# h turned by a transposing DMA in place of TensorE, six slots for the split halves, and a scalar operand for the bound on y

## What is computed

```python
h = jnp.maximum(_layernorm(x, axis=-1), 0.0)          # x: (6144, 128)
anchor_adj = jnp.einsum('md,de,ne->mn', h, weight, input)
scores = jnp.where(adj > 0, anchor_adj, NEG_PAD)      # adj: (6144, 6144) int32
atten = jax.nn.softmax(scores / TEMPERATURE, axis=1)
return x + atten @ input                              # input: (6144, 128)
```

## Time and profile before

| | us |
|---|---|
| median of three runs | 934.15 |
| the profiled execution | 933.88 |
| its span, first to last instruction | 932.1 |
| PE busy | 914.1 (98%) |
| DVE busy | 820.8 (88%) |
| ACT busy | 747.8 (80%) |
| POOL busy | 660.8 (71%) |

### The profile page before, as it was taken

The page is one execution under the profiler, slowest core; times in us unless marked ns, Lnnn a source line. Parts: engine busy times, 40 slices in busy tenths (PEclk is TensorE's granted clock), DMA queues, the critical chain, the costliest instruction groups (busy, mean ns, idle before and its releaser), DMA issues.

```text
span 932.1 us, 25954 instructions
## 1 busy us (share of the span) xinstructions
PE 914.1 (98%) x7611; PEld 663.4 (71%) x7611; DVE 820.8 (88%) x1670; ACT 747.8 (80%) x1511; POOL 660.8 (71%) x449
## 2 busy tenths in 40 slices
PE   7979999999999999999999999999999999999997
PEld 4457777777777777777777777777777777777776
DVE  7988889888988898888988899889888888888885
ACT  5858878888888888888888888888888888888885
POOL 5998677767776776677677767776777677767712
PEclk9999999999999999999999999999999999999999
DMA  9789999999999999999999999999999999999955
GB/s 348 224 219 247 274 250 282 268 259 276 256 272 264 267 268 267 264 262 267 268 263 269 260 269 270 267 256 269 269 269 250 275 270 267 254 267 270 267 99 99
DMA packets 347401, 239.51 MB, mean 257 GB/s; under 512 B 308848, under 2 KB 327408, under 8 KB 328944
## 3 DMA queue, kind: packets, MB, share of 16 engines
q1 hardware_dynamic: 340176, 235.92, 98.0%
q10 hardware_dynamic: 7200, 3.28, 1.3%
HBM read 160.50 MB, written 3.15 MB: 176 GB/s over the span
## 4 chain that ended last, share of the span: by engine, by line
PE 94%; DVE 3%; DMA 2%; issue 1%; ACT 0%; POOLq 0%; POOL 0%; SPq 0%; DVEq 0%; ACTq 0%
PE ps_s L842 39%; PE ps_o L889 26%; PE ps_o L891 13%; PE ps_t L865 13%; DMA pT_dma<-split 1%; DVE probs L643 1%; PE ps_t L908 1%; PE ps_s L918 1%; PE ps_s L835 1%; DVE v L710 1%; DVE pT_lo L666 0%; DMA nodes_raw<-in_L_gnn_input_dram 0%; DVE split L672 0%; PE ps_o L908 0%; ACT yT_hi L544 0%
## 5 line engine op out<-in xcount | busy, mean ns | idle before, releaser
L643 DVE CUSTOM_DVE_ANT_0 probs<-ps_s,absent 128x1024 f32<-128x1024 f32 x288 | 351.5, 1221 | 43.6 <-PE ps_s L842 38.5
L415 POOL TENSOR_SCALAR absent<-present 128x2048 bf16<-128x2048 bf16 x143 | 299.2, 2092 | 66.6 <-DVE chunk_max L643 40.2
L406 POOL TENSOR_SCALAR present<-adj_i 128x2048 bf16<-128x2048 int32 x144 | 272.7, 1894 | 31.1 <-DMA adj_i<-in_adj_dram 25.8
L539 ACT ACTIVATE pT_hi<-ps_t 128x512 f16<-128x512 f32 x281 | 167.7, 597 | 145.7 <-PE ps_t L865 145.5
L889 PE MATMUL ps_o<-v,pT_dma 128*128 128x256 f16 x1152 | 221.0, 273 | 2.0 <-DMA pT_dma<-split 1.9
L507 ACT ACTIVATE ps_t<-probs,neg_max,exp_scale 128x512 f32<-128x512 f32 x285 | 220.4, 773 | 2.5 <-DVE neg_max L653 1.2
L666 DVE TENSOR_TENSOR pT_lo<-ps_t,pT_hi 128x512 f16<-128x512 f32 x284 | 194.5, 685 | 28.7 <-ACT pT_hi L539 28.0
L842 PE MATMUL ps_s<-yT_hi,hT_hi 128*128 128x512 f16 x576 | 218.6, 380 | 1.1 <-DVE chunk_max L643 0.9
L842 PE MATMUL ps_s<-yT_lo,hT_hi 128*128 128x512 f16 x576 | 218.7, 380 | 0.0
L889 PE MATMUL ps_o<-v,pT_hi 128*128 128x256 f16 x1152 | 206.2, 273 | 5.4 <-DVE v L710 4.6
L891 PE MATMUL ps_o<-v,pT_dma 128*128 128x128 f16 x1152 | 205.6, 219 | 0.0
(11 more groups left out here) (81 smaller groups left out, 608.7 us busy)
## 6 DMA issues: line engine op xcount, KB each, us to landing
adj_i<-in_adj_dram SPq DMA_DIRECT2D x144, 1024.0 KB, 5.3
pT_dma<-split SPq DMA_TRANSPOSE x288, 3.4
nodes_raw<-in_L_gnn_input_dram SPq DMA_DIRECT2D x6, 512.0 KB, 6.3
x_res<-in_x_dram SPq DMA_DIRECT2D x48, 64.0 KB, 5.0
out_dram<-fin ACTq DMA_DIRECT2D x48, 64.0 KB, 2.3
x_ln<-in_x_dram SPq DMA_DIRECT2D x46, 64.0 KB, 5.0
x_ln<-in_x_dram ACTq DMA_DIRECT2D x2, 64.0 KB, 3.0
w<-in_L_gnn_weight_dram SPq DMA_DIRECT2D x1, 64.0 KB, 2.1
```

Of the source, the lines that this page charges most:

```text
L406: nc.gpsimd.tensor_scalar(flags(s, c), adj_i[:, c, :], 1.0, 0.0, ALU.min, ALU.max)\
L415: nc.gpsimd.tensor_scalar(by_block(absent[:, c, :]), by_row(flags(s, c)), -ABSENT, ABSENT, ALU.mult, ALU.add).then_inc(absent_done, 1)
L539: nc.scalar.activation(pT_hi[:, p % BANKS, :], turn_area(k, at), ACT.Copy).then_inc(hi_done, 1)
L643: nc.vector.tensor_tensor_reduce(out=probs[:, s, j * SCORE:(j + 1) * SCORE], in0=ps_s[j % 2][:, :], in1=absent[:, c, part * SCORE:(part + ...
```

## The change

h of tiles 0 and 1 is still turned by PE. From tile 2 on POOL makes h with the relu in it (`h_centred`, then `h`), splits it into two fp16 parts (`split_h`, two instructions) and SP turns both parts with one transposing DMA of 256 columns, behind the D halves 2 and 3 of the step, in the queue ahead of the load of adj. PE's scores of tile t+2 wait for that DMA. `turn_h`, `hi_h` and `lo_h` leave the steps. `split` gets six slots, and the waits for a slot change. `y_bound` is made by an operation with a scalar operand.

```diff
+        split = sb("split", [P, D_HALVES, 2, TURN], fp16)
         pT_dma = sb("pT_dma", [P, D_HALVES, 2 * PER_TURN, P], fp16)
-        hT_hi = sb("hT_hi", [P, 2, P], fp16)
-        hT_lo = sb("hT_lo", [P, 2, P], fp16)
+        hT = sb("hT", [P, 2, 2, P], fp16)
+        h_centred = sb("h_centred", [P, 2, D], fp32)
         h = sb("h", [P, 2, D], fp32)
+        h_split = sb("h_split", [P, 2, 2, D], fp16)
         x_ln = sb("x_ln", [P, 2, D], fp32)
         x_res = sb("x_res", [P, 2, D], fp32)
         fin_a = sb("fin_a", [P, 2, D], fp32)
...
             return u * 8 + (16 - 8 * s)
+        def h_turns(u, s):
+
+            return u * 8 - 8 * s
+
         def evac(t, n, at=None):
...
+                sp.dma_start_transpose(pT_dma[:, d, :, :], split[:, d, :, :].rearrange("p s n -> p (s n)"))\
                     .then_inc(turned_in[d], 16)
...
                     turn_d(t, 2, g, late(at, 0, g) if at == LAST else evac(t, g - 2))
+                if has(at, 2):
+
+                    sp.wait_ge(scores_made, t * SCORES + SCORES)
+                    sp.sem_inc(sp_waited, 1)
+                    sp.wait_ge(h_split_done, t + 1)
+                    sp.sem_inc(sp_waited, 1)
+                    sp.dma_start_transpose(hT[:, par, :, :], h_split[:, par, :, :].rearrange("p s n -> p (s n)"))\
+                        .then_inc(hT_in[par], 16)
                 next_adj(0)
...
-            def make_h(u, s, free):
+            def make_h(u, s):
                 pool.wait_ge(aggr_done, u + 1)
                 pool.sem_inc(pool_waited, 1)
                 nc.gpsimd.tensor_scalar(var_eps[:, s, :], mean_var[:, s, 1:2], EPS, H_SCALE ** -2, ALU.add, ALU.mult)\
...
                 nc.gpsimd.tensor_tensor(rstd[:, s, :], var_eps[:, s, :], minus_half[:, :], ALU.pow)\
                     .then_inc(rstd_done, 1)
                 pool.wait_ge(rstd_done, u + 1)
-                if free:
+                pool.sem_inc(pool_waited, 1)
+                nc.gpsimd.tensor_scalar(h_centred[:, s, :], x_ln[:, s, :], mean_var[:, s, 0:1], 0.0,
+                                        ALU.subtract, ALU.max).then_inc(h_centred_done, 1)
+                pool.wait_ge(h_centred_done, u + 1)
+                if isinstance(u, int) and u in (2, 3):
+
                     pool.wait_ge(h_turned, u - 1)
                 pool.sem_inc(pool_waited, 1)
-                nc.gpsimd.tensor_scalar(h[:, s, :], x_ln[:, s, :], mean_var[:, s, 0:1], rstd[:, s, :],
-                                        ALU.subtract, ALU.mult).then_inc(h_done, 1)
+                nc.gpsimd.tensor_scalar(h[:, s, :], h_centred[:, s, :], rstd[:, s, :], 1.0, ALU.mult, ALU.mult)\
+                    .then_inc(h_done, 1)
+
+            def split_h(u, s):
+                pool.wait_ge(h_done, u + 1)
+                if not (isinstance(u, int) and u < 4):
+
+                    pool.wait_ge(hT_in[s], h_turns(u - 2, s))
+                pool.sem_inc(pool_waited, 1)
+                nc.gpsimd.tensor_scalar(h_split[:, s, 0, :], h[:, s, :], 1.0, 1.0, ALU.mult, ALU.mult)\
+                    .then_inc(h_hi_done, 1)
+                pool.wait_ge(h_hi_done, u - 1)
+                nc.gpsimd.tensor_tensor(h_split[:, s, 1, :], h[:, s, :], h_split[:, s, 0, :], ALU.subtract)\
+                    .then_inc(h_split_done, 1)
             def flags(s, c):
...
-                pool.wait_ge(turned_in[(d + BANKS) % D_HALVES], LAST * 16 + (16 if d >= BANKS else 0))
+                pool.wait_ge(turned_in[d], LAST * 16)
                 pool.sem_inc(pool_waited, 1)
-                nc.gpsimd.tensor_scalar(split[:, d % BANKS, 0, :], part, 1.0, 1.0, ALU.mult, ALU.mult)\
+                nc.gpsimd.tensor_scalar(split[:, d, 0, :], part, 1.0, 1.0, ALU.mult, ALU.mult)\
                     .then_inc(split_hi_done, 1)
                 pool.wait_ge(split_hi_done, d // 2 + 1)
-                nc.gpsimd.tensor_tensor(split[:, d % BANKS, 1, :], part, split[:, d % BANKS, 0, :],
+                nc.gpsimd.tensor_tensor(split[:, d, 1, :], part, split[:, d, 0, :],
                                         ALU.subtract).then_inc(split_done, 1)
-            make_h(0, 0, False)
...
-            make_h(2, 0, True)
+            make_h(2, 0)
+            split_h(2, 0)
             v_lo_pool(0)
             pool.wait_ge(absent_done, 4)
...
-                    make_h(t + 3, 1 - par, True)
+                    make_h(t + 3, 1 - par)
+                    split_h(t + 3, 1 - par)
                     convert(t + 3, 1 - par, 0, True)
                 if at == LAST - 1:
...
-                if not (isinstance(u, int) and u < 2):
-                    act.wait_ge(scores_made, u * SCORES - SCORES)
-                nc.scalar.activation(hT_hi[:, s, :], ps_s[s if isinstance(u, int) and u < 2 else 0][:, 0:P],
-                                     ACT.Relu).then_inc(hT_hi_done, 1)
+                nc.scalar.activation(hT[:, s, 0, :], ps_s[s][:, 0:P], ACT.Copy).then_inc(hT_hi_done, 1)
             def exp_p(u, s, c):
                 act.wait_ge(neg_max_done, u + 1)
...
-                if d >= BANKS:
-                    act.wait_ge(turned_in[d - BANKS], u * 16 + 16)
-                elif not (isinstance(u, int) and u == 0):
-                    act.wait_ge(turned_in[d + BANKS], u * 16)
-                nc.scalar.activation(split[:, d % BANKS, 0, :], ps_t[n % BANKS][:, :], ACT.Copy)\
+                if not (isinstance(u, int) and u == 0):
+                    act.wait_ge(turned_in[d], u * 16)
+                nc.scalar.activation(split[:, d, 0, :], ps_t[n % BANKS][:, :], ACT.Copy)\
                     .then_inc(hi_done, 1)
             def v_hi(i):
...
-                            hi_h(t + 2, par)
                         for g in range(1 if at is not None and at + ahead == LAST else 2):
                             hi_d(t + ahead, c, g, CYCLE * z + 2 + g)
-                    elif z == 0 and has(at, 2):
-                        hi_h(t + 2, par)
             steps(act, step)
             act.wait_ge(fin_done, TILES)
...
-                nc.vector.scalar_tensor_tensor(out=hT_lo[:, s, :], in0=area[:, 0:P], scalar=0.0,
-                                               in1=hT_hi[:, s, :], op0=ALU.max, op1=ALU.subtract)\
+                nc.vector.tensor_tensor(hT[:, s, 1, :], area[:, 0:P], hT[:, s, 0, :], ALU.subtract)\
                     .then_inc(hT_lo_done, 1)
...
-                nc.vector.tensor_tensor(split[:, d % BANKS, 1, :], ps_t[n % BANKS][:, :], split[:, d % BANKS, 0, :],
+                nc.vector.tensor_tensor(split[:, d, 1, :], ps_t[n % BANKS][:, :], split[:, d, 0, :],
                                         ALU.subtract).then_inc(turn_freed, 1)
...
-                nc.vector.tensor_tensor(y_bound[:, :], nodes_top[:, :], w_top[:, :], ALU.mult)\
+                nc.vector.tensor_scalar(y_bound[:, :], nodes_top[:, :], w_top[:, :], None, ALU.mult)\
                     .then_inc(y_bound_done, 1)
                 dve.wait_ge(y_bound_done, 1)
...
-                                if has(at, 2):
-                                    lo_h(t + 2, par, ps_s[0])
                                 find_max(t + ahead, (par + ahead) % 2)
                         if q == 0:
                             lo_p(t, CYCLE * z + 1, at)
...
-                part, y, q = ((hT_hi, yT_hi, 0), (hT_hi, yT_lo, 0), (hT_hi, yT_hi, 1), (hT_hi, yT_lo, 1),
-                              (hT_lo, yT_hi, 0), (hT_lo, yT_hi, 1))[i]
+                part, y, q = ((0, yT_hi, 0), (0, yT_lo, 0), (0, yT_hi, 1), (0, yT_lo, 1),
+                              (1, yT_hi, 0), (1, yT_hi, 1))[i]
                 cols = slice(j * SCORE + q * 512, j * SCORE + (q + 1) * 512)
-                made = nc.tensor.matmul(ps_s[j % 2][:, q * 512:(q + 1) * 512], part[:, s, :], y[:, cols],
-                                        start=(part is hT_hi and y is yT_hi), stop=(part is hT_lo))
+                made = nc.tensor.matmul(ps_s[j % 2][:, q * 512:(q + 1) * 512], hT[:, s, part, :], y[:, cols],
+                                        start=(part == 0 and y is yT_hi), stop=(part == 1))
                 if i == 5:
                     made.then_inc(scores_made, 1)
...
-                        pe.wait_ge(hT_lo_done, t + 3)
+                        pe.wait_ge(hT_in[par], h_turns(t + 2, par))
                     for i in range(6):
...
-                    if z == 0 and has(at, 2):
-                        pe.wait_ge(masked, t * SCORES + (SCORES + 5))
-                        turn_h(t + 2, par, ps_s[0])
                     for q in range(2, CYCLE):
                         product(t, par, k + q, at)
```

More of the change, by code:

```diff
@@ L116, in gnn_masked_attention_kernel @@
         pT_lo = sb("pT_lo", [P, BANKS, TURN], fp16)
-        split = sb("split", [P, BANKS, 2, TURN], fp16)
+        split = sb("split", [P, D_HALVES, 2, TURN], fp16)
         pT_dma = sb("pT_dma", [P, D_HALVES, 2 * PER_TURN, P], fp16)
-        hT_hi = sb("hT_hi", [P, 2, P], fp16)
-        hT_lo = sb("hT_lo", [P, 2, P], fp16)
+        hT = sb("hT", [P, 2, 2, P], fp16)
```

(18 more changed lines are left out.)

## The result

The changed kernel takes 972.41 us (median of four runs, 969.99 to 974.99) against 934.0: 1.0403 of before, 95% interval 1.0379 to 1.0427. It is 38 us slower. The forecast was 962, with a range of 943 to 986. The profiled execution took 973.09 us, with a span of 971.3.

What follows compares the result with a forecast made beforehand. PE's own order was taken to bound the kernel. Late landing of h (26.1 us) plus early steps (3) less the bound on y (0.9) gave 28.2 us on 933.88, so 962 us, range 943 to 986.

Steps and rivals of the forecast that it cites:

- What bounds the kernel: Whole kernel: PE is dense in steps of 18.52 us, 0.18 of it for h, and only PE's order sets the steps.
- The new path decides: PE's scores of tile t+2: h lands by DMA 0.58 us late, step 19.10, 26.1 us over 45 steps; own case 0.68.
- The 3 us for early steps: Steps 1 to 6, where the queue is behind and h lands later: 3 us added, out of a possible 8.
- The bounds of the landing: Turning DMA of h, issue to landing: between 1.8 us (order behind the large transpose) and 3.05 us (equal time); 2.15 taken.
- the faster rival: At PE's scores of tile t+2: h lands in time, 9.2 us come off, 925 us; chance 0.09.
- SP's load of adj behind the new DMA: In SP's list: the load of adj is issued at most 0.9 us later, costing nothing while the queue keeps up.
- that rival: The 16 DMA engines become the bound: adj 0.9 us later pushes everything behind it in 46 steps, 41 us, 975; chance 0.12.
- GpSimd: Making and splitting h on GpSimd: 1.1 us more per step, upper end 3.3, hidden by its 2.81 us wait for the mean.
- Slots and bound: Six slots: nothing, as PE does not wait there in dense steps; y_bound with a scalar operand: 0.9 us less.
- The rest of my signs: Expected in the changed profile: PE waits about 0.76 us at first scores, PE's share below 98%, DMA issued 4.8 us after `finish`.

Runs made afterwards that it cites:

- the run with half of adj: The changed kernel with only half of each piece of adj loaded from the fourth tile on, giving the DMA queue slack: 966.3 us, 1.0341 of before.
- the run at 929: The changed kernel with the turning DMA of h issued at the head of SP's step, ahead of the pair for D halves 2 and 3: 929.0 us, 0.9942.
- the run that took 963 us: The changed kernel with h turned by PE as before; the turning DMA stays in its place ahead of adj, into an unread tile: 963.1 us, 1.0318.

## Why the prediction was right, and where it was off

*What bounds the kernel.* Right: PE's order sets the steps, and at 18.35 us a step it does so with h gone from it.

*The new path decides.* Right in mechanism, shown by the change's chain and by the run with half of adj, where the wait alone keeps the step at 19.24 against 19.10 predicted. Of its terms: from `finish` to the issue 4.88 us against 4.82; from issue to landing 2.28 against 2.15; landing to PE 0.05 (462.31 to 462.36) against 0.14. Together 7.21 against 7.11. The rest of the step is 12.03 against 11.99. Over 45 steps the 0.14 are 6 of the 10 us between 962 and 972, and the drop of the clock and the long wait near 887 some 3. The 3 us for early steps held: from the first `finish` to the eleventh the changed kernel takes 195.5 us (67.18 to 262.69) against 185.5 (67.06 to 252.56), 2.8 more than ten steps by 0.72.

*The bounds of the landing.* Both held. In the step shown the large transpose ahead, issued at 458.41 with 3.5 us to landing, is in at 461.9, and h at 462.31, 0.4 behind it, so order in the queue was the right reason against the faster rival, as far as this step shows it. The Trainium skill's figure of 1309 ns for a turn by DMA ("VectorE: DVE Perf Modes", The three transpose paths) is for one bf16 block of 128x128; the two fp16 blocks here took 2.3 us at best from issue to landing, which is what a consumer sees. The rule of the Trainium skill (same page, Rules for kernel authors), TensorE where PSUM will do, agrees with the change's 972. With the same DMA at the head of the step, at 0.9942, it does not show: PE's own turn, with slots and bound, gives 0.9963, and the two intervals overlap.

*SP's load of adj behind the new DMA: "0.9 at most", "Nothing, while the queue keeps up".* This is the step that failed, though the time does not show it. I took a quarter of the large transpose's issue time for a quarter of the columns. The instructions on hT say otherwise (ns min/median/max):

```profile
L368 SPq DMA_TRANSPOSE hT<-h_split x46: 1167/1168/1178, 49.0 to 925.2; - x46
```

1.17 us to issue 256 columns, where 1024 take 1.24 to 1.28. So adj is issued 6.36 us after `finish` (455.15 to 461.51) in place of 4.82, 1.54 later and not 0.9, and the queue does not keep up. The forecast held this for a rival, at 0.12 and 975 us; the measured one is 963, in steps of 19.03. It is not an alternative to PE's wait but lies under it. Without the wait, but with the queue's order left, 963 remains: less than 10 of the 38 us come back.

*The argument against that rival*, that landings fell from 4.7 to 3.4 while the step was 18.52, was too weak. It shows that the queue drains in the order of before. It says nothing of an order in which the engines run empty first.

*GpSimd.* Its groups by form, in ns of one:

```profile
L409 POOL TENSOR_SCALAR h_centred<-x_ln,mean_var 128x128 f32<-128x128 f32 x48 | 34.6, 721 | 10.1 <-POOL rstd L405 10.1
...
L428 POOL TENSOR_TENSOR h_split<-h,h_split 128x128 f16<-128x128 f32 x46 | 19.9, 432 | 3.8
L416 POOL TENSOR_SCALAR h<-h_centred,rstd 128x128 f32<-128x128 f32 x48 | 18.1, 378 | 9.9 <-POOL h_centred L409 9.9
L425 POOL TENSOR_SCALAR h_split<-h 128x128 f16<-128x128 f32 x46 | 13.8, 299 | 12.4 <-POOL h L416 12.4
```

1.83 us where one of 0.80 was, and some 0.6 of idle time before the last three, so 1.6 more against the 1.1 I took, within my 3.3. It is hidden, as forecast: the run at 929 has it too. My sign for it was wrong: GpSimd's wait for the mean did not fall by 1.1 but rose, from 117.4 to 139.4 us in 43 waits, for the step grew by 0.7 and other waits of GpSimd went (40.2 us for VectorE's masking before and next to nothing after; for adj 25.8 before and 9.0 after).

*Slots and bound.* The bound's 0.9 fits its operation (1.02 to 0.22 us) and its interval of 0.5 to 3.3 us, which reaches further; "nothing" for the slots is neither shown nor excluded. In the change the 0.9 is not seen at the first `finish`, at 67.18 against 67.06.

*The rest of my signs* held: the wait at the first scores (0.86 a step against 0.76), PE's share at 94% (below 98%), the issue 4.9 us after `finish` where 4.8 was forecast.

## What to carry to other kernels

When work moves to a queue, follow two chains: from the last thing that the new transfer stands behind to the one who waits for it, and from the transfer to what stands behind it in the list. Where a queue is nearly full, the second can cost as much as the first and hide under it, so undo the two one at a time. A wait as large as the loss is not yet the cause of all of it.

## What the runs showed of the hardware that I had not expected

A transpose of 256 columns takes SP 1.17 us to issue, one of 1024 columns 1.24 to 1.28; a plain DMA takes 0.33 to 0.37 in the steps shown. The issue is nearly a fixed cost here, while the landing does follow size in part (2.3 against 3.0 to 3.6 us).

With the queue late, the issue itself of a large transpose takes longer, 3.00 us in place of 1.24 in the run that took 963 us. (Single ones do so elsewhere: the longest in the kernel before took 3.50.) In SP's timeline the second of a pair is:

```profile
472.09 3.00 SPq L349 DMA_TRANSPOSE pT_dma<-split  x1
475.44 1.17 SPq L370 DMA_TRANSPOSE hT_spare<-h_split  x1
```

So a late queue also makes SP late, and SP issues adj late, which leaves the engines at 0.58 again. By this the slow order can keep itself up, though the same bytes in another order fit into a step of 18.35 us. That the late issue is the link in this loop is an inference from the timeline; no run changed it alone.
